# Order within the queues of a two-layer transformer kernel: z_lo behind w, the turn of cw, maxima ahead of hid_lo, score banks

## Time and profile before

| | |
|---|---|
| median of 3 runs | 886.93 us (885.39 to 888.92) |
| the profiled execution | 885.39 us, span 883.7 us |
| PE busy | 825.5 us, 93% |
| DVE busy | 659.3 us, 75% |
| ACT busy | 519.3 us, 59% |
| POOL busy | 468.9 us, 53% |
| mean granted clock of TensorE | 0.984 |
| chain that ended last | PE 64%, issue 12%, DVE 12%, POOL 9%, ACT 3% |

### The profile page before, as it was taken

One profiled execution on the slowest core, in us unless ns is written; L12 is line 12 of the kernel. 1 busy time (PEld: TensorE's weight loads), 2 busy tenths in 40 slices (PEclk: granted clock), 3 DMA queues, 4 the chain that ended last, 5 costly groups with the idle time before them and its releaser, 6 DMA issues.

```text
span 883.7 us, 14685 instructions
## 1 busy us (share of the span) xinstructions
PE 825.5 (93%) x4500; PEld 625.8 (71%) x4500; DVE 659.3 (75%) x1354; ACT 519.3 (59%) x1099; POOL 468.9 (53%) x400
## 2 busy tenths in 40 slices
PE   4899999999999999878998999999999988999997
PEld 3678888778688888656787888654444446888886
DVE  5799999999988999788376865866777643576554
ACT  3688888778788888562544533354566564454442
POOL 3556666666456565533666776531300524566774
PEclk9999999999999999999999999978999999999999
DMA  4223222222332222112665458312431123334441
GB/s 141 104 96 97 96 95 95 96 96 86 127 96 96 95 95 96 48 67 73 206 221 180 137 156 281 116 57 75 130 132 50 55 74 114 117 122 139 149 155 66
DMA packets 57857, 99.97 MB, mean 113 GB/s; under 512 B 8320, under 2 KB 19072, under 8 KB 57792
## 3 DMA queue, kind: packets, MB, share of 16 engines
q1 hardware_dynamic: 57792, 99.17, 33.9%
HBM read 72.67 MB, written 9.57 MB: 93 GB/s over the span
## 4 chain that ended last, share of the span: by engine, by line
PE 64%; issue 12%; DVE 12%; POOL 9%; ACT 3%; DMA 1%; DVEq 0%; POOLq 0%; ACTq 0%; SPq 0%
PE ps L917 9%; PE ps L894 9%; PE ps L903 8%; PE ps L319 6%; PE ps L382 4%; PE ps L330 4%; PE ps L370 3%; POOL q_sin L515 3%; PE ps L1585 3%; PE ps L1555 3%; PE ps L343 3%; PE ps L1468 3%; PE ps L357 2%; PE ps L1489 2%; DVE nm L1779 2%
## 5 line engine op out<-in xcount | busy, mean ns | idle before, releaser
L1044 POOL TENSOR_TENSOR ew_lo<-ew_raw,ew_hi 128x768 fp32r<-128x768 f32 x68 | 127.7, 1879 | 69.3 <-ACT ew_hi L1009 41.3
L991 ACT ACTIVATE hid_hi<-guw 128x512 fp32r<-128x512 f32 x68 | 43.0, 632 | 160.2 <-POOL guw L1060 108.0
L1060 POOL TENSOR_TENSOR guw<-gu,cwb 128x512 f32<-128x512 f32 x64 | 84.7, 1324 | 98.2 <-issue 73.8
L1099 DVE TENSOR_TENSOR hid_lo<-guw,hid_hi 128x512 fp32r<-128x512 f32 x68 | 78.7, 1158 | 76.1 <-ACT hid_hi L991 76.0
L1779 DVE TENSOR_REDUCE nm<-ps 128x1 f32<-128x512 f32 x128 | 81.3, 684 | 24.7 <-PE ps L1489 24.5
L1674 ACT ACTIVATE e<-ps 128x512 f32<-128x512 f32 x128 | 69.0, 598 | 38.4 <-PE ps L1585 38.0
L502 DVE SCALAR_TENSOR_TENSOR w<-ex,rden,sgn 128x512 f32<-128x512 f32 (+3 forms) x128 | 90.9, 772 | 0.0
L430 ACT ACTIVATE ex<-sabs,nmax 128x512 f32<-128x512 f32 (+3 forms) x128 | 61.5, 552 | 43.1 <-DVE nmax L476 43.1
L515 POOL TENSOR_TENSOR q_sin<-q_sw,sin 128x512 f32<-128x512 f32 x64 | 85.0, 1348 | 1.4 <-DMA q_sw<-q_in 1.2
L917 PE MATMUL ps<-ew_hi,hid_hi 128*128 128x256 f32 x272 | 78.6, 289 | 5.9 <-DVE hid_lo L1099 4.4
L917 PE MATMUL ps<-ew_lo,hid_hi 128*128 128x256 f32 x272 | 77.2, 284 | 0.0
(11 more groups left out here) (181 smaller groups left out, 2403.9 us busy)
## 6 DMA issues: line engine op xcount, KB each, us to landing
ew_raw<-in_ew SPq DMA_DIRECT2D x68, 384.0 KB, 3.2
q_sw<-q_in SPq DMA_DIRECT2D x128, 128.0 KB, 2.0
cwb<-cw_dram SPq DMA_DIRECT2D x64, 256.0 KB, 3.7
wqk_raw<-in_wqk SPq DMA_DIRECT2D x32, 256.0 KB, 2.6
wv_raw<-in_wv SPq DMA_DIRECT2D x32, 128.0 KB, 2.6
wo_raw<-in_wo SPq DMA_DIRECT2D x32, 128.0 KB, 2.1
qs<-stk_q SPq DMA_DIRECT2D x16, 256.0 KB, 3.5
ks<-stk_k SPq DMA_DIRECT2D x16, 256.0 KB, 4.1
```

Source lines behind the costliest of these rows:

```text
L1044: pool.tensor_tensor(ff[f].ew[1][:, i % EW_SLOTS, :], ew_raw[:, i % RAW_SLOTS, :], fp(ff[f].ew[0][:, i % EW_SLOTS, :]), ALU.subtract).then ...
L1060: pool.tensor_tensor(ff[f].guw[:, i % 2, :], ff[f].gu[:, i % 2, :], ff[f].cwb[:, r % CWB_SLOTS, :], ALU.mult).then_inc(sem("guw"), 1)
L1099: dve.tensor_tensor(ff[f].hid[1][:, i % 2, :], ff[f].guw[:, i % 2, :], fp(ff[f].hid[0][:, i % 2, :]), ALU.subtract).then_inc(sem("hid_lo"), 1)
```

## The change

It does five things.

1. In `a0_dve` the instruction z_lo of head i moves from before the four w of head i + 1 to behind them.
2. At step N0 `cw_turn` moves ahead of up of item 2; its bank is 4 instead of 0, and it waits for gate_half of item 1 instead of for the additions to x. gate of item 3, which uses bank 4 next, waits for cwT; the wait for cwT in row 4 goes. On VectorE `ln_stats` moves ahead of `gated` of item 1.
3. At the end of layer 0's experts, VectorE's two maxima (tiles 24 and 25) move ahead of the last hid_lo.
4. The three score banks are taken in the order 0, 1, 3 instead of 3, 0, 1, and all wait for both additions to x.
5. The high part of the maxima is made by a copy instead of by a maximum of a tile with itself.

```diff
@@ a0_dve
-            if valid(i, N0):
-                n = i
-                wait(dve, "z_hi", n + 1)
-                dve.tensor_tensor(z0[1][:, :], ps[:, 7, :], fp(z0[0][:, :]), ALU.subtract).then_inc(sem("z_lo"), 1)
             if valid(i + 1, N0):
                 n = i + 1
                 wait(dve, "rden", n + 1)
...
                 for qi in QORDER:
                     dve.scalar_tensor_tensor(out=w[:, qi, ROW[qi]], in0=ex[:, qi, ROW[qi]], scalar=rden[:, qi:qi + 1],
                                              in1=sgn[:, par(1), qi, ROW[qi]], op0=ALU.mult, op1=ALU.mult).then_inc(sem("w"), 1)
+            if valid(i, N0):
+                n = i
+                wait(dve, "z_hi", n + 1)
+                dve.tensor_tensor(z0[1][:, :], ps[:, 7, :], fp(z0[0][:, :]), ALU.subtract).then_inc(sem("z_lo"), 1)
@@ a0_at_pe, a0_at_dve
                 gate(pe, 0, 2)
+                cw_turn(pe, 0, 0)
                 up(pe, 0, 2)
-                cw_turn(pe, 0, 0)
...
             if i == N0:
+                ln_stats(dve, 1, 1)
                 gated(dve, 0, 1)
-                ln_stats(dve, 1, 1)
@@
-        CWT_BANK = {(0, 0): 0, (0, 1): 1, (1, 0): 7, (1, 1): 3}
+        CWT_BANK = {(0, 0): 4, (0, 1): 1, (1, 0): 7, (1, 1): 3}
@@ cw_turn
             if (f, h) == (0, 0):
-                pe.wait_ge(sem("x_add"), 4)
+                silu_done(pe, f, 2)
@@ gate
+            if (f, i) == (0, 3):
+                wait_f(pe, f, "cwT", 1)
@@ row_pe
             if (f, i) == (0, T1_AT[0]):
-                wait_f(pe, f, "cwT", 1)
                 ln_pe(pe, 1, (1,))
@@ ffn_dve
-            hid_low(dve, f, NI - 1)
             if f == 0:
                 a1_row_dve(dve, NI, 0)
+            hid_low(dve, f, NI - 1)
             y_to_x(dve, f, 1)
@@
-        S_BANK = (3, 0, 1)
+        S_BANK = (0, 1, 3)
@@ a1_pe
-                if n == 0:
-                    pe.wait_ge(sem("max"), HEADS * (LEAD - 1) + 1)
-                elif n < S_BANKS:
-                    pe.wait_ge(sem("x_add"), 6 + n)
...
+            pe.wait_ge(sem("x_add"), 8)
+            pe.wait_ge(sem("max"), HEADS * (LEAD - 1) + 1)
             for n in range(S_BANKS):
                 scores(n)
@@ maximum_dve
-                dve.tensor_tensor(nm_s[:, quad % 2, 0:16], nm1[:, quad % 2, :], nm1[:, quad % 2, :], ALU.max).then_inc(sem("nm_hi"), 1)
+                dve.tensor_copy(nm_s[:, quad % 2, 0:16], nm1[:, quad % 2, :]).then_inc(sem("nm_hi"), 1)
```

## The result

| | before | after |
|---|---|---|
| median of 4 runs each, on the same chip | 886.16 us (881.72 to 888.92) | 897.0 us (893.17 to 904.01) |
| ratio of after to before | | 1.0146, 95% interval 1.01 to 1.0192 |
| the profiled execution | 885.39, span 883.7 | 899.52, span 897.8 |
| PE busy, granted clock | 825.5, 0.984 | 831.5, 0.979 |
| DVE, ACT, POOL busy | 659.3, 519.3, 468.9 | 646.5, 519.6, 466.0 |

The changed kernel is 10.8 us slower by the medians; 893.8 was forecast, in a range of 888.5 to 900. The spans of the two profiles differ by more, 14.1 us.

A forecast was written before the change was run, and what follows sets the result against it. TensorE was taken to bound the first attention's head loop (period 11.04 us), with VectorE 95% busy beside it. Terms 2.7 + 2.3 + 1.9 + 0 = +6.9 gave 892.3 on the profiled basis, 893.8 as a median; range 888.5 to 900.

The forecast's parts named there:

- the upper case of the prediction (3.5): Plain heads, edit 1: stall 0.16 a head, costing 3.5 us if POOL's chain is not shortened; expected 0.03 a head, 0.7.
- the cover in the last heads: Last heads, edit 1: o stalls 0.9 to 1.5 longer, hidden by TensorE's later 2.02 wait for q_rot; cost 0.
- rows 2: Profile rows of a first-attention head in the kernel before: period 11.04 us, the four w taking 2.96 around POOL's wqk_lo.
- Edit 2 (forecast 2.3): Turn of cw: waits for item 1's gate_half, runs 2.3 us later behind 3.5 idle; the shift carries on.
- The wait of 2.64: TensorE's wait for hid_lo at 418.84; hid_lo hangs on the delayed cw chain, so the 2.3 is carried on.
- Edits 3 and 4 (forecast 1.9): Seam of the layers: maxima delay hid_lo and down by 1.53, first exp comes 2.66 later; 1.9 taken between.
- the one that hid the exp's extra: At 590.25 TensorE waits 0.53 for VectorE's maxima, which carries the 1.53 and a little, mostly hiding the exp's extra.
- The sentence on the two ports: Maxima, edit 5: a copy gets two read ports, so could be shorter but still held by POOL; sum unaffected.
- still blocked: Rival, every head: POOL gets in before the last w, stall 0.7 a head, 15 us in 22 heads: 908; chance 0.06.
- VectorE sets the pace: Rival, head loop: VectorE sets the period, so shorter w blocks give up to 28.8 us back: 864; chance 0.05.
- absorbed: Rival: adding heads at low end, plain heads free, half the cw shift absorbed, seam 1.5; 3.55 in all, 890.5; chance 0.17.
- The clock: Rival, seam of the layers: new stalls put 6 us more of products at half clock, adding 3 us: 896.8; chance 0.08.

The follow-up runs named there:

- but1: The changed kernel with edit 1 undone (z_lo ahead of w again); ratio to the kernel before 1.0108 (1.0069 to 1.0147).
- scal5: The kernel before with the eight maxima for the high part made by a tensor_scalar (times 1.0); ratio 1.001 (0.9972 to 1.0048).
- only2: The kernel before with edit 2 alone (turn of cw and ln_stats moved ahead); ratio 1.0062 (1.0017 to 1.0107).
- but5: The changed kernel with edit 5 undone (maximum again instead of copy); ratio to the kernel before 1.0101 (1.0065 to 1.0137).
- after2: The changed kernel once more, all five edits; ratio to the kernel before 1.0129 (1.0081 to 1.0177).
- only34: The kernel before with edits 3 and 4 alone (maxima ahead of last hid_lo; score banks and waits); ratio 1.0029 (0.9985 to 1.0073).
- only3: The kernel before with edit 3 alone (two maxima ahead of the last hid_lo); ratio 1.0029 (0.9998 to 1.0061).
- only5: The kernel before with edit 5 alone (copy for maximum, eight times); ratio 1.0004 (0.9966 to 1.0041).
- sel1: The kernel before with z_lo behind w only in the two head loops and at steps 14 to 18; ratio 1.0021 (0.9984 to 1.0057).

## Why the prediction was right, and where its sizes were not

**Edit 1 (forecast 2.7).** The mechanism was right at four of five places: plain heads, first heads, heads with additions and the change of batch. The shifts of T and o in the changed kernel against the profile of before, taken apart: 0.6 from the start of the program, 0.6 in the first heads (forecast 0, up to 0.9), 2.4 in the loops, 2.2 in the heads with additions (3.3), −1.1 at the change of batch (−1.25), 1.75 in the last heads (0, "1.5 if that cover is gone"). The sum is 6.5. In the heads with additions the low end held, twice 1.1, and o waited 1.47 there, not 2 to 3. Two terms were mis-sized. The stall in a plain head is nearer 0.1 than 0.03, with a few of 0.2 to 0.4 as each loop settles, so the upper case of the prediction (3.5) was the nearer one. And the cover in the last heads was too thin: against two waits of 2.1 for z_lo, and the half clock with them, q_rot gave back 1.5 (2.02 to 0.56) and 0.8 at its other place.

What the prediction did not have at all is on the other side: the kernel before pays more for the blocked w in some executions. The prediction took rows 2, with one w left, for every plain head; a plain head with two left cost TensorE 0.9 to 1.3, and the two of but1 with three left 2.6 and 2.9. Over the eight executions with z_lo early the last o came 0, 0.1, 3.2, 3.6, 4.3, 6.7, 9.3 and 11.2 late, 4.8 in the mean; over the four with z_lo late in every head 6.5, 7.5, 8.0 and 8.5, 7.6 in the mean. So edit 1 costs some 2.8 in the mean. With a spread of 4 among eight draws this is no better than ±3, and it leans on single profiles of different kernels: counted from T of the first head it is 2.5, and without scal5, itself a long run, 3.5. That it equals the forecast's 2.7 is luck: two errors of opposite sign. For the same reason the profile was a poor stand-in for the median: on the four other chips of the experiments the kernel before had medians of 889.0 to 893.7, 3.6 to 8.3 above its profiled 885.39.

**Edit 2 (forecast 2.3).** Right: idle 3.57 before the turn, 2.3 by which it is late, in the changed kernel and in only2, and 0.5 against 1.8 for its two halves. The wait of 2.64 ended with the delayed chain, as the prediction had it, and swallowed nothing. The shift grew to 2.6 behind the turn; what added the 0.3 no run takes apart.

**Edits 3 and 4 (forecast 1.9).** down late by 1.6 (1.53), the first exp by 2.8 (2.66): right. The step that failed is the one that hid the exp's extra: at the next transposes the whole 2.5 was there, in the changed kernel and in but1 and but5 (2.5 each), and 3.8 in after2, at a lower clock. Whether it stays depends on the clock of the next 20 us: in only34 and only3 about 3 were given back, in after2 2.4 more were added.

**Edit 5 (forecast 0, ends ±2.4).** The row of 304 ns was a mean of six of about 0.18 and two of 0.68 and 0.65, and the last stood beside POOL's ew_lo. There the copy took 4.16 to 4.19 in 3 of 4 executions; in the changed kernel and in only5 what followed was 1.9 to 2.6 late. The sentence on the two ports in the prediction, from the Trainium skill, VectorE: DVE Perf Modes, section "Mode 2×_2P — use both read ports for one tensor", is not decided by it: scal5, one source as well, took 0.62.

**The sum.** 2.8 + 2.6 + 2.5 + three quarters of 2.3 = 9.6, against 10.8 and 10.7 by the medians of the two comparisons, and 12.9 and 11.5 by their ratios. The rest is within their intervals. Without edit 1 the sum is 6.8, and but1 has 9.6 (6.1 to 13.1) by its ratio. So the waits of each part are shown, but the runs cannot tell whether edit 1 costs anything in the mean. Of the rivals, "still blocked" and "VectorE sets the pace" are refuted by w at 1.94 and by the slower result, "absorbed" by edits 2 to 4, though its low end for the heads with additions came true. "The clock" was a part: at the last heads, and at the seam of after2 and only34. It is no pure effect of the new stalls: with z_lo early, only34, only5 and sel1 too were short of 1.7 us of clock near 380.

## What to carry to other kernels

One profiled execution is one draw. Where two engines contend for something exclusive at almost the same moment, compare several executions of the same code before pricing an edit there, and read the largest member of a group, not its mean. Read the members one by one, too: the length of a held block says how many were still to come when the other engine began. An instruction that takes its turn behind others inherits their bad cases: z_lo behind w took over w's in the heads where POOL adds. And an edit that makes a stage steadier may still be slower than the mean of what it replaces.

## What the runs showed of the hardware

Where several VectorE instructions wait on a row of POOL instructions, in the heads they went in turn: one w behind each POOL instruction. The four w took 1.93 with none left when POOL began, 2.96 with one, 3.99 with two, 4.98 with three, with the same code in the heads. POOL waited in its turn: q_sin took 1.46 behind the last w and 1.29 without one (95.98 and 97.40 in the kernel before). Beside the three ew_lo the turn was not sure: a single copy took 0.63 in one execution and 4.16 to 4.19 in three, the maximum 0.61 to 0.65 in eight and 2.40 in one, all starting 1.20 to 1.24 behind the first ew_lo. The Trainium skill, SBUF — State Buffer, section "Who interferes with whom", says that who starts first keeps the pair of ports for its whole instruction. The runs agree with that, and show beyond it that one who waits usually gets the next turn and can be passed over. What tells the two cases apart is not shown.

The stretch at the lower of TensorE's two clocks (granted 0.50, which is 1.2 of 2.4 GHz) behind the seam, where TensorE has waited for the last hid_lo and for x, was of chance length too: of the 60 us from 580 to 640 TensorE was short of full clock by 3.4 us in only3, 8.5 before and 13.7 in after2. In six executions whose seam is that of before and which differ in edits elsewhere, it was 5.1 to 10.2.
